# An LSTM recurrence over 10,000 rows, cut into chunks: from one group of 250 columns to two groups of 125 that take turns

## The reference

```python
h  = item_feat @ W_item.T + b_item
x  = x + relu(adj @ h + layernorm(x) @ W_user.T + b_user)

xp = layernorm(x) @ W_ih.T + b_ih + b_hh
def step(carry, xp):                      # over the 10,000 rows, in order
    h, c = carry
    i, f, g, o = split(xp + h @ W_hh.T, 4)
    c = sigmoid(f) * c + sigmoid(i) * tanh(g)
    h = sigmoid(o) * tanh(c)
    return (h, c), h
logits = hs @ W_lin.T + b_lin
g   = argmax(logits)                      # 0 or 1 for each row
w   = g * hs
inc = cumsum(w)
x   = x + 2 * hs + (inc - w) * fw_att + (inc[-1] - inc) * bw_att
```

## Time and profile before

| | |
|---|---|
| median of 3 runs | 1634.55 us (1634.08 to 1634.62) |
| the profiled execution | 1634.17 us |
| its span, first to last instruction | 1632.3 us |
| TensorE busy | 1493.0 us (91%) |
| VectorE busy | 1281.2 us (78%) |
| ScalarE busy | 1136.2 us (70%) |
| GpSimd busy | 250.6 us (15%) |
| bytes moved | 426.61 MB |

### The profile page before, as it was taken

How to read it: one execution, slowest core, us unless ns; L and a number is a source line. 1 busy time by engine, 2 the same in 40 slices (tenths; PEclk the granted TensorE clock), 3 DMA queues, 4 the chain that set the end, 5 groups by cost and what they waited for, 6 DMA issues and landing times.

```text
span 1632.3 us, 25593 instructions
## 1 busy us (share of the span) xinstructions
PE 1493.0 (91%) x7104; PEld 1233.8 (76%) x7104; DVE 1281.2 (78%) x2049; ACT 1136.2 (70%) x1786; POOL 250.6 (15%) x267
## 2 busy tenths in 40 slices
PE   6999999999999999999999999999967777788882
PEld 5878888888888888878888788888856666677662
DVE  5988878888888888888888888888845555677777
ACT  4677777777777777777777777777745555556551
POOL 0000000000000000000000000000012112366665
PEclk9999999999999999999999999999989999999996
DMA  9789999999999999999999999999730000000003
GB/s 373 258 310 361 357 366 356 358 361 347 361 357 367 362 353 361 344 358 360 366 360 353 359 347 363 363 363 362 291 133 0 0 0 0 0 0 0 0 0 126
DMA packets 70072, 426.61 MB, mean 261 GB/s; under 512 B 8674, under 2 KB 17698, under 8 KB 69540
## 3 DMA queue, kind: packets, MB, share of 16 engines
q1 hardware_dynamic: 68320, 425.12, 68.9%
q10 hardware_dynamic: 1732, 1.24, 0.3%
HBM read 416.09 MB, written 10.24 MB: 261 GB/s over the span
## 4 chain that ended last, share of the span: by engine, by line
issue 79%; PE 9%; DVE 6%; ACT 4%; DVEq 1%; POOL 0%; ACTq 0%; POOLq 0%
PE psZ L656 8%; DVE H L887 3%; ACT gt L496 2%; ACT u_hi L489 1%; ACT th L500 1%; DVE y L993 1%; DVE ig L876 1%; DVE C L880 0%; DVEq L900 0%; POOL rstd L346 0%; DVEq L908 0%; POOLq L349 0%; DVEq L871 0%; DVE gh L858 0%; ACTq L499 0%
## 5 line engine op out<-in xcount | busy, mean ns | idle before, releaser
L738 DVE TENSOR_TENSOR a_lo<-raw,a_hi 128x1000 fp32r<-128x1000 f32 (+1 forms) x800 | 907.3, 1181 | 132.3 <-ACT a_hi L448 129.0
L448 ACT ACTIVATE a_hi<-raw 128x1000 fp32r<-128x1000 f32 (+1 forms) x800 | 803.2, 1028 | 204.2 <-PE psG L582 185.0
L580 PE MATMUL psG<-a_hi,item_hi 128*128 128x500 f32 (+1 forms) x1580 | 637.6, 404 | 11.6 <-DVE a_lo L738 11.5
L582 PE MATMUL psG<-a_hi,item_lo 128*128 128x500 f32 (+1 forms) x1580 | 617.2, 391 | 0.0
L581 PE MATMUL psG<-a_lo,item_hi 128*128 128x500 f32 (+1 forms) x1580 | 614.6, 389 | 0.0
L580 PEld LDWEIGHTS psG<-a_hi,item_hi 128*128 128x128 f32 (+1 forms) x1580 | 297.5, 188 | 92.5 <-DVE a_lo L738 21.7
L582 PEld LDWEIGHTS psG<-a_hi,item_lo 128*128 128x128 f32 (+1 forms) x1580 | 298.6, 189 | 61.5
L581 PEld LDWEIGHTS psG<-a_lo,item_hi 128*128 128x128 f32 (+1 forms) x1580 | 298.3, 189 | 61.0 <-issue 4.4
L496 ACT ACTIVATE gt<-psZ 128x250 f32<-128x250 f32 (+1 forms) x440 | 137.5, 338 | 167.3 <-PE psZ L656 160.0
L656 PE MATMUL psZ<-H,wh 128*128 128x250 f32 x704 | 172.5, 388 | 81.5 <-DVE H L887 80.3
L346 POOL TENSOR_TENSOR rstd<-var,minus_half 125x4 f32<-125x4 f32 x40 | 74.4, 1860 | 1114.2 <-DVE var L722 1114.2
(11 more groups left out here) (96 smaller groups left out, 816.4 us busy)
## 6 DMA issues: line engine op xcount, KB each, us to landing
raw<-in_adj_main SPq DMA_DIRECT2D x360, 1000.0 KB, 5.7
raw<-in_adj_main SPq DMA_DIRECT2D x40, 750.0 KB, 4.1
x_copy<-xb SPq DMA_DIRECT2D x20, 250.0 KB, 5.2
x<-x_copy SPq DMA_DIRECT2D x1, 5000.0 KB, 15.5
out<-y SPq DMA_DIRECT2D x25, 200.0 KB, 2.1
xb<-in_xT SPq DMA_DIRECT2D x18, 250.0 KB, 5.3
u<-in_itemT SPq DMA_DIRECT2D x3, 1024.0 KB, 18.9
u<-in_itemT SPq DMA_DIRECT2D x1, 904.0 KB, 24.4
```

Of the source, the lines that this page charges most:

```text
L448: nc.scalar.activation(a_hi[:, s % CUT, 0:n], raw[:, r % RAW, at:at + n], ACT.Copy)\
L580: pe.matmul(bank, w_hi, hi, start=(c == 0), stop=False)
L582: last = pe.matmul(bank, w_lo, hi, start=False, stop=(c == CH))
L738: dve.tensor_tensor(a_lo[:, s % CUT, 0:n], raw[:, r % RAW, at:at + n], a_hi[:, s % CUT, 0:n].bitcast(f32), ALU.subtract).then_inc(lo_ready, 1)
```

## The change

The recurrence is written anew, and the rest is left.

- **Groups.** The 250 chunks become two groups, A and B, of 125 columns. Each engine's step does A, then B, interleaved, with semaphores of their own for each group.
- **Input term.** `u_hi`, `u_lo`, `wx_hi` and `wx_lo` are gone. TensorE multiplies in float32 with `wx` and streams the stepped columns of `u` itself (`from_input`), for the next step, behind both groups' state terms (`from_state`).
- **Steps.** W = 40, so 80 steps. The first chunks, which have no 40 rows ahead of them, get other rows copied in, and chunk 0's outputs are computed in a side path (`h_head`, `gh_head`, `cum_head`, `y_head`).
- **Places.** A gate pair is 250 columns of one bank, one tanh for two gates; tanh of i and f, their product with `C`, and tanh of `C` are written to PSUM (`tb`). The states of all main steps stay in `hist`, contiguous for each step.
- **Sums.** Gating (`gate`), the scalings (`scale_gated`, `scale_run`) and POOL's additions (`sums`, `write_y`) work on two steps at a time; `own` and its product move from VectorE to ScalarE and POOL.

```diff
 K = 250
 L = N // K
-W = 48
+W = L
 STEPS = W + L
-KH = K // 2
-XC = 256
-assert K % 2 == 0 and XC - K <= W
+KG = K // 2
+HL = L // 2
+PAIRS = L // 2
 OUTS = 25
 OW = N // OUTS
 HANDOVER_TOL = 2.0 ** -19
-assert OW % L == 0 and W % 2 == 0 and L % 2 == 0
-CELL = 2
-GATES = (1, 0, 2, 3)
+assert K * L == N and OW % L == 0 and L % 8 == 0 and OW >= 3 * L
+Z_BANK = (0, 2)
+T_BANK = (4, 5)
+D_BANK = (6, 7)
...
+        def zb(g, bank):
+            return psZ[:, Z_BANK[g] + bank, 0:2 * KG]
+        def tb(g, j, n=1):
+            return psZ[:, T_BANK[g], j * KG:(j + n) * KG]
...
-            def lstm(n, par, first_two=False, main=0):
-                if not first_two:
-                    pe.wait_ge(t_ready, 5 * n - 5)
-                    pe.wait_ge(u_lo_ready, n - 1)
-                else:
-                    pe.wait_ge(first_lo_ready, n + 1)
-                for q in GATES:
-                    if main == 3 and q == GATES[-1]:
-                        pe.wait_ge(gated, n - W - 1)
-                    w_hi, w_lo = (w[:, q * HID:(q + 1) * HID] for w in (wx_hi, wx_lo))
-                    bank = psZ[:, 4 * par + q, 0:XC]
-                    pe.matmul(bank, w_hi, u_hi[:, par, :], start=True, stop=False)
-                    pe.matmul(bank, w_hi, u_lo[:, par, :], start=False, stop=False)
-                    pe.matmul(bank, w_lo, u_hi[:, par, :], start=False, stop=False)
-                pe.wait_ge(h_ready, 2 * n + 1)
-                for q in GATES:
-                    pe.matmul(psZ[:, 4 * par + q, 0:K], wh[:, q * HID:(q + 1) * HID], H[:, par, :],
-                              start=False, stop=True).then_inc(z_ready, 1)
-                if main >= 2:
-                    logits(par)
-            def logits(par):
-                pe.matmul(psZ[:, 4 * (1 - par) + GATES[-1], XC:XC + K], wd[:, :], H[:, par, :],
+            def from_input(n, g, wait=True, alone=False):
+                cols_in = u[:, ds(n + g * KG * L, KG, L)]
+                for bank in range(2):
+                    if wait:
+                        pe.wait_ge((t0_ready, t1_ready)[bank][g], n)
+                    for j in range(2):
+                        q = 2 * bank + j
+                        last = pe.matmul(zb(g, bank)[:, j * KG:(j + 1) * KG], wx[:, q * HID:(q + 1) * HID], cols_in,
+                                         start=(j == 0), stop=alone, skip_group_check=True)
+                    if alone:
+                        last.then_inc((z0_ready, z1_ready)[bank][g], 1)
+            def from_state(n, g, row):
+                pe.wait_ge(h_ready[g], n)
+                for bank in range(2):
+                    for j in range(2):
+                        q = 2 * bank + j
+                        last = pe.matmul(zb(g, bank)[:, j * KG:(j + 1) * KG], wh[:, q * HID:(q + 1) * HID],
+                                         hist[:, row, g * KG:(g + 1) * KG], start=False, stop=True,
+                                         skip_group_check=True)
+                    last.then_inc((z0_ready, z1_ready)[bank][g], 1)
+            def logits(row, par, half):
+                pe.matmul(psZ[:, D_BANK[par], half * K:(half + 1) * K], wd[:, :], hist[:, row, :],
                           start=True, stop=True).then_inc(d_ready, 1)
 
-            pe.wait_ge(prep, 14)
+            def lstm(n, row, more=True):
+                from_state(n, 0, row)
+                from_state(n, 1, row)
+                if more:
+                    from_input(n + 1, 0)
+                    from_input(n + 1, 1)
+            def lstm_pair(i, par, more=True):
+                for half in range(2):
+                    n = W + 2 * i + half + 1
+                    from_state(n, 0, 2 * i + half)
+                    from_state(n, 1, 2 * i + half)
+                    if half == 0 and not (isinstance(i, int) and i < 2):
+                        pe.wait_ge(gated, i - 1)
+                    logits(2 * i + half, par, half)
+                    if more or half == 0:
+                        from_input(n + 1, 0)
+                        from_input(n + 1, 1)
...
+            def gates(n, g):
+                act.wait_ge(z0_ready[g], n + 1)
+                nc.scalar.activation(tb(g, 0, 2), zb(g, 0), ACT.Tanh).then_inc(t0_ready[g], 1)
+                act.wait_ge(z1_ready[g], n + 1)
+                nc.scalar.activation(go[:, g, :], zb(g, 1), ACT.Tanh).then_inc(t1_ready[g], 1)
+            def cell_tanh(n, g):
+                act.wait_ge(c_ready[g], n + 1)
+                nc.scalar.activation(tb(g, 3), group(C, g), ACT.Tanh, scale=0.5).then_inc(th_ready[g], 1)
+            def scale_gated(i, par):
+                act.wait_ge(gated, i + 1)
+                if not (isinstance(i, int) and i < 2):
+                    act.wait_ge(own_ready, i - 1)
+                nc.scalar.activation(mgh[:, par, :, :], gh[:, par, :, :], ACT.Copy, scale=mbw[:, 0:1])\
+                    .then_inc(mgh_ready, 1)
+            def scale_run(i, par):
+                act.wait_ge(run_ready, 2 * i + 2)
+                if not (isinstance(i, int) and i < 2):
+                    act.wait_ge(y_ready, i - 1)
+                nc.scalar.activation(run_c[:, par, :, :], run[:, par, :, :], ACT.Copy, scale=dfb[:, 0:1])\
                     .then_inc(run_c_ready, 1)
 
+            def lstm(n, extra=None):
+                gates(n, 0)
+                gates(n, 1)
+                cell_tanh(n, 0)
+                if extra is not None:
+                    extra()
+                cell_tanh(n, 1)
+            def lstm_pair(i, par):
+                lstm(W + 2 * i + 3, lambda: scale_gated(i, par))
+                lstm(W + 2 * i + 4, lambda: scale_run(i, par))
...
+            def products(n, g):
+                dve.wait_ge(t0_ready[g], n + 1)
+                dve.scalar_tensor_tensor(tb(g, 2), tb(g, 1), 1.0, group(C, g), ALU.add, ALU.mult)\
+                    .then_inc(parts[g], 1)
+                dve.wait_ge(t1_ready[g], n + 1)
+                dve.scalar_tensor_tensor(ig[:, g, :], tb(g, 0), 1.0, go[:, g, 0:KG], ALU.add, ALU.mult)\
+                    .then_inc(parts[g], 1)
+            def cell(n, g):
+                dve.wait_ge(parts[g], 2 * n + 2)
+                dve.scalar_tensor_tensor(group(C, g), tb(g, 2), 0.5, ig[:, g, :], ALU.mult, ALU.add)\
+                    .then_inc(c_ready[g], 1)
+            def state(n, g, row):
+                dve.wait_ge(th_ready[g], n + 1)
+                dve.scalar_tensor_tensor(hist[:, row, g * KG:(g + 1) * KG], go[:, g, KG:2 * KG], 1.0, tb(g, 3),
+                                         ALU.add, ALU.mult).then_inc(h_ready[g], 1)
+            def lstm(n, row):
+                products(n, 0)
+                cell(n, 0)
+                products(n, 1)
+                state(n, 0, row)
+                cell(n, 1)
+                state(n, 1, row)
+            def gate(i, par):
+                dve.wait_ge(d_ready, 2 * i + 2)
+                if not (isinstance(i, int) and i < 2):
+                    dve.wait_ge(run_ready, 2 * i - 1)
+                    dve.wait_ge(mgh_ready, i - 1)
+                d = psZ[:, D_BANK[par], 0:2 * K].rearrange("p (s k) -> p s k", k=K)
+                dve.scalar_tensor_tensor(gh[:, par, :, :], d, thr[:, 0:1], hist[:, ds(2 * i, 2), :],
+                                         ALU.is_gt, ALU.mult).then_inc(gated, 1)
+            def lstm_pair(i, par):
+                lstm(W + 2 * i + 2, 2 * i + 2)
+                gate(i, par)
+                lstm(W + 2 * i + 3, 2 * i + 3)
+            with nc.vector.Fori(0, W // 4) as i:
+                for r in range(4):
...
+            def write_y(i, par):
+                pool.wait_ge(run_c_ready, i + 1)
+                pool.wait_ge(own_ready, i + 1)
+                rows = y[:, :].rearrange("p (k l) -> p l k", l=L)[:, ds(2 * i, 2), :]
+                pool.tensor_tensor(rows, own[:, par, :, :], run_c[:, par, :, :], ALU.add).then_inc(y_ready, 1)
+            def sums(i, par, reset=False):
+                pool.wait_ge(gated, i + 1)
+                if reset:
+                    pool.memset(run[:, par, 0, 0:3:2], 0.0).then_inc(run_reset, 1)
+                    pool.wait_ge(run_reset, 1)
+                pool.tensor_tensor(run[:, par, 1, :], run[:, par, 0, :], gh[:, par, 0, :], ALU.add)\
                     .then_inc(run_ready, 1)
+                pool.wait_ge(run_ready, 2 * i + 2)
+                if not (isinstance(i, int) and i == 0):
+                    pool.wait_ge(run_c_ready, i)
+                pool.tensor_tensor(run[:, 1 - par, 0, :], run[:, par, 1, :], gh[:, par, 1, :], ALU.add)\
+                    .then_inc(run_ready, 1)
+                if not (isinstance(i, int) and i == 0):
+                    write_y(i - 1, 1 - par)
+                rows = x1[:, :].rearrange("p (k l) -> p l k", l=L)[:, ds(2 * i, 2), :]
+                pool.tensor_tensor(base[:, :, :], hist[:, ds(2 * i, 2), :], rows, ALU.add).then_inc(base_ready, 1)
+                pool.wait_ge(base_ready, i + 1)
```

(74 more changed lines are left out.)

398 lines of the change are left out of this document (176 added, 222 removed).

## The result

The changed kernel takes 1700.28 us (median of 4 runs, 1698.90 to 1702.15) against 1634.32 for the kernel before (4 runs, 1631.73 to 1634.62): ratio 1.0408, 95% interval 1.0390 to 1.0426. It is slower by 4.1%; 1532 was forecast, faster, and the time lies outside the range. It lies 7 us above the price of rival 1 (1693).

The account below looks back on a forecast made before the run. One step's chain was taken as the bound, no engine being full. Span 1632.3 - 102.5 (steps) - 2.8 (start) + 3.0 (end) = 1530.0, + 1.9 + 0.4 = 1532 us; range 1515 to 1605, 8 in 10.

Parts of the forecast that it names:

- rival 1: Input matmuls in the recurrence: the stepped read of u stretches TensorE, kernel slower, 1693 us; 17 of 100.
- the strided operand: Input matmuls streaming u at a step of 40 elements: taken to cost nothing, bounds up to +161 us.
- ScalarE's absolute 1.92 ns a column: Bound for stepped input matmuls: a record of 0.240 us, +161 us in all.
- The break-even of 0.193 us a record: Input matmuls: 0.082 us more a record, 1.54 ns a column, would use up the 102.3 us gain.
- VectorE's +0.68 ns: Bound for stepped input matmuls: VectorE's extra per column on TensorE's 0.87 ns, put at about 1631 us.
- TensorE's load: Recurrence step: 32 records at 0.111 us, 3.55 us in the warm-up; 3.97 in the main part with logits.
- The chains and the turns: Two groups alternate in a step: A's state at 3.04 us, B's near 4.0, both covered by TensorE's load.
- The lock: VectorE's state operations beside POOL: with one operand in PSUM, nothing charged for POOL running beside the recurrence.
- the gain of this edit alone: Operand in PSUM, were POOL to block: 0.63 us a step, inside the slack and a little over it.
- The other engines: Main step: VectorE 2.8 us, ScalarE 2.9 to 3.4, POOL 6.8 per two steps; all below TensorE.
- Start and end: Before and after the recurrence: start -2.8 us (0 to -4), end +3 us (1 to 6).
- Rivals 2 and 3: Recurrence: chain or wait replaces TensorE as limit, 1571 us, 18 of 100; groups don't overlap, 1610, 3 of 100.

Follow-up runs that it names:

- The run of other steps: Kernel of its own without the computation: each engine runs groups of equal operations on resident data at several steps between columns; 455.11 us as a whole.
- the version with rows: Changed kernel, but POOL copies each row's stepped columns once into hist and TensorE streams neighbours; 1530.53 us, ratio 0.9374 to the kernel before.

## Why the prediction was wrong

**The step that failed** is one sentence of the part on the strided operand: "I take nothing, since TensorE's own row shows twice the feed it needs." The premise was that float32 "asks for data at half the rate at which it can be fed". That feed was measured on neighbouring columns, and says nothing of stepped ones. The term was not 0 but (0.245 - 0.111) x 16 x 78 = 167 us. The dearest of the bounds, ScalarE's absolute 1.92 ns a column, was 161; TensorE's 1.94 to 1.97 is 1 to 3% above it. The break-even of 0.193 us a record was right: with 0.245 the kernel had to be slower. One price beside it was a slip: VectorE's +0.68 ns on 125 columns is 0.085 us a record, 1532 + 106 = 1638 and not 1631, so that price too was on the slower side. Rival 1 had all of it, priced at 1693, and got 17 in 100. What was wrong was to let an argument on spare rate outweigh two rows of this very tensor, read with this very step, on two engines, both of which showed a price.

By the Trainium skill ("SBUF — State Buffer", Specifications), which wants two hits in each line of 16 bytes for full bandwidth, the input term is stretched, and the trace agrees: 0.245 us against 0.111. The run of other steps agrees with it for float32 (free at step 2, between at 3, double from 4). It disagrees with the same page's note on cachelines, which lets 4 float32 or 8 bf16 elements be strided for free: float32 pays at step 3 (0.169 against 0.114 us) and at 4, and bf16 at step 4, with two elements in a line, is doubled (7.5 against 3.8 us). The measurement decides.

**TensorE's load otherwise**: right. State records 0.113 against 0.111; with straight input records the step is 3.57 against 3.55, and from first to last state matmuls it is 295.0 us (1493.56 - 1198.59 by the timeline of that run) against 292.9.

**The chains and the turns**: right, and needed. A's state was forecast at 3.04 us after the start and B's near 4.0; the version with rows has 2.96 (1300.97 + 0.28 - 1298.29) and 3.89. Writing to PSUM cost nothing that mattered. Taking turns is worth 36 us.

**The lock**: right in charging nothing. The state operation takes 285 ns (273 to 290 over 160) also where POOL runs. But "the gain of this edit alone, 0.63 us a step, would be inside the slack and a little over it" was too low: with the gates in SBUF four operations of each group are held off, not the last one, and the run lost 68 us, 1.45 in each main step and 8.5 in the warm-up.

**The other engines**: all below TensorE, as said, and lighter. POOL's five operations of two steps take 1.49, 1.26, 1.25, 0.72 and 0.72 us by their means in the groups of the changed kernel from 1500 to 1660 us, 5.4 together and not 6.8; the bound was no worse for being generous.

**Start and end**: small errors that partly cancel. State matmuls of step 1 were forecast near 1201.0, they came at 1202.45 (the inputs of steps 0 and 1 are stepped too), and at 1198.59 with straight reads. The timeline row of `total` in the changed kernel, which answers to the earlier trace rows:

```profile
1678.86 0.16 DVE L1112 SCALAR_TENSOR_TENSOR total<-cum,mbw 128x1 f32<-128x1 f32 x1 [1.16 <-issue]
```

From the last state matmuls to it there are 1678.86 - 1665.35 = 13.5 us, as in the kernel before (13.6), and the output after it takes 21.4 (1700.3 - 1678.86) instead of 19.5. So the end grew by 1.8 us and not by the 3.0 forecast. Together the forecast with the right price is 1532 + 167 = 1699, against 1700.28; so small a difference owes something to errors of opposite sign.

**The rivals**: rival 1 is shown. Rivals 2 and 3 fall: TensorE is never idle in the recurrence.

## What to carry to other kernels

A copy that looks like mere preparation may be what turns a stepped operand into a straight one; without it each matmul pays for the step on the engine that sets the pace, so let an idle engine gather such columns once. Where a resource has no row for a new access pattern, price it by the rows of other engines on the same data, in nanoseconds an element, before arguing from spare rate. If those bounds straddle the break-even point, no forecast should put 8 in 10 on one side of it.
